# Cross-attention and feed-forward on one core: the order of the start of the attention phase is changed

## The reference

```python
x = x + xattn(layernorm(x), ctx_768, Wq, bq, Wk, bk, Wv, bv, Wo, bo)
x = x + ffn(layernorm(x), W1, b1, phases, w_real, w_imag, W2, b2)
# xattn: q = h@Wq+bq; k, v = ctx@Wk+bk, ctx@Wv+bv; 16 heads of 32
#   attn = softmax(clip(q k^T * 32**-0.5, -1e4, 1e4)); if any value is NaN: attn = 1/64 everywhere
#   (attn v) @ Wo + bo
# ffn: hidden = h@W1+b1; imag = w_imag*sin(phases + 0.1*hidden)
#   q = hidden + (cos(phases)*w_real + sin(phases)*w_imag)*imag*0.1;  relu(q)@W2 + b2
```

## Time and profile before

| | us |
|---|---|
| median of 3 runs (lowest, highest) | 2076.57 (2076.09, 2077.97) |
| profiled execution, its time | 2075.65 |
| profiled execution, span from first to last instruction | 2073.9 |
| mean granted clock of TensorE in it | 0.994 |
| busy in it: TensorE, VectorE | 2046.1, 1360.8 |
| busy in it: ScalarE, GpSimd | 1146.1, 1041.5 |

### The profile page before, as it was taken

The page is one execution under the profiler, slowest core; times in us unless marked ns, Lnnn a source line. Parts: engine busy times, 40 slices in busy tenths (PEclk is TensorE's granted clock), DMA queues, the critical chain, the costliest instruction groups (busy, mean ns, idle before and its releaser), DMA issues.

```text
span 2073.9 us, 27093 instructions
## 1 busy us (share of the span) xinstructions
PE 2046.1 (99%) x9738; PEld 1719.5 (83%) x9738; DVE 1360.8 (66%) x2037; ACT 1146.1 (55%) x2037; POOL 1041.5 (50%) x754
## 2 busy tenths in 40 slices
PE   6999999999999999999999999999999999999999
PEld 5888888888888888888888888888888888888887
DVE  6888888888876765555555555555656556565554
ACT  4666767767664655454554545545455444554543
POOL 3767777777776345344343433435434353343521
PEclk9899999999999999999999999999999999999999
DMA  5123223223213321211112111121111211112100
GB/s 183 57 77 104 90 82 113 82 87 97 72 62 111 114 76 37 72 41 41 44 49 71 41 41 41 51 72 41 41 41 52 71 41 41 41 48 75 37 26 21
DMA packets 133654, 133.93 MB, mean 65 GB/s; under 512 B 68872, under 2 KB 84744, under 8 KB 133520
## 3 DMA queue, kind: packets, MB, share of 16 engines
q1 hardware_dynamic: 132512, 132.16, 21.3%
q10 hardware_dynamic: 1008, 0.04, 0.0%
HBM read 81.83 MB, written 50.35 MB: 64 GB/s over the span
## 4 chain that ended last, share of the span: by engine, by line
PE 92%; DVE 3%; ACT 2%; issue 1%; DMA 1%; POOL 1%; SPq 0%; POOLq 0%; ACTq 0%; DVEq 0%
PE psum L1168 29%; PE psum L1170 29%; PE psum L1169 29%; PE psum L1251 3%; PE psum L1174 1%; DVE hid L1100 1%; DMA x_dram<-res 0%; ACT act_hi L836 0%; DVE act_lo L1103 0%; ACT hid L847 0%; POOL prob L606 0%; ACT frac L832 0%; DMA x_sb<-in_x 0%; ACT w_hi L684 0%; POOL q_lo L559 0%
## 5 line engine op out<-in xcount | busy, mean ns | idle before, releaser
L658 POOL TENSOR_TENSOR frac<-turns,frac 128x512 f32<-128x512 f32 x256 | 333.3, 1302 | 827.7 <-DVE frac L1128 827.7
L1100 DVE SCALAR_TENSOR_TENSOR hid<-frac,gain,hid 128x512 f32<-128x512 f32 x256 | 322.4, 1259 | 143.5 <-ACT frac L832 142.4
L1168 PE MATMUL psum<-w_hi,act_hi 128*128 128x512 f32 x1024 | 398.4, 389 | 0.9 <-DVE act_lo L1103 0.9
L1170 PE MATMUL psum<-w_hi,act_lo 128*128 128x512 f32 x1024 | 398.4, 389 | 0.0
L1169 PE MATMUL psum<-w_lo,act_hi 128*128 128x512 f32 x1024 | 398.3, 389 | 0.0
L836 ACT ACTIVATE act_hi<-hid 128x512 fp32r<-128x512 f32 x256 | 161.8, 632 | 356.3 <-DVE hid L1100 356.3
L845 ACT ACTIVATE turns<-psum,u_shift 128x512 f32<-128x512 f32 x256 | 176.5, 689 | 327.3 <-PE psum L1170 269.1
L1103 DVE SCALAR_TENSOR_TENSOR act_lo<-hid,act_hi 128x512 fp32r<-128x512 f32 x256 | 197.6, 772 | 178.8 <-ACT act_hi L836 178.8
L1128 DVE TENSOR_SCALAR frac<-turns 128x512 f32<-128x512 f32 x256 | 111.4, 435 | 248.5 <-ACT turns L845 248.5
L1168 PEld LDWEIGHTS psum<-w_hi,act_hi 128*128 128x128 f32 x1024 | 192.2, 188 | 41.0 <-issue 1.3
L1170 PEld LDWEIGHTS psum<-w_hi,act_lo 128*128 128x128 f32 x1024 | 192.3, 188 | 39.8
(11 more groups left out here) (158 smaller groups left out, 4199.8 us busy)
## 6 DMA issues: line engine op xcount, KB each, us to landing
res<-in_x SPq DMA_DIRECT2D x64, 256.0 KB, 2.9
x_dram<-res SPq DMA_DIRECT2D x64, 256.0 KB, 2.0
x_sb<-in_x SPq DMA_DIRECT2D x15, 1024.0 KB, 5.8
x_sb<-x_dram SPq DMA_DIRECT2D x15, 1024.0 KB, 5.6
xn<-turn_dram SPq DMA_DIRECT2D x30, 512.0 KB, 5.9
out<-x_sb SPq DMA_DIRECT2D x15, 1024.0 KB, 5.8
turn_dram<-stage SPq DMA_DIRECT2D x112, 128.0 KB, 2.4
stage<-in_w SPq DMA_DIRECT2D x32, 256.0 KB, 2.9
```

The lines of the kernel that those rows point to most:

```text
L658: pool.tensor_tensor(frac[:, j % 2, :], turns[:, j % 2, :], frac[:, j % 2, :], ALU.subtract)\
L1100: dve.scalar_tensor_tensor(out=hid[:, j % 2, :], in0=frac[:, j % 2, :], scalar=gain[:, f:f + 1], in1=hid[:, j % 2, :], op0=ALU.mult, op1=A ...
L1168: pe.matmul(o, a_hi, b_hi, start=first, stop=False)
L1170: return pe.matmul(o, a_lo, b_hi, start=False, stop=last)
```

## The change

- The sums of the context (for the mean value) are no longer taken from PSUM ahead of wk's low parts. They are taken in step 1 (`SUM_STEP`), one sum over the high parts and one over the low parts in SBUF, and added; a new tile `ctx_rest` holds the second. The small products of step 5 wait for them.
- wq's high parts are made by ScalarE, one behind each high part of tile 0, and no more by VectorE.
- keys(1) comes ahead of queries(0), values(0) behind it, both ahead of step 0; the other values move up a step. values(2) and values(3) use other banks, and waits on banks are renamed to fit.
- ScalarE takes keys_rows(1) and wv's high parts ahead of q_to_hi(0).
- VectorE reduces the phases and writes the rows of values(0) ahead of step 0, the phases in the same operations as before.
- The norm of tile 1 on ScalarE stands behind q_to_hi(2) and the exponential of step 1.
- wo's first block is split in step 3.

```diff
--- before.py
+++ after.py
@@ -99,8 +99,9 @@
 
 
 K_BANKS, K_STEPS = (2, 3, 7, 5), (None, None, 0, 1)
-V_BANKS, V_STEPS = (2, 6, 7, 6), (0, 1, 2, 3)
-WO_STEPS = (4, 4, 5, 5)
+V_BANKS, V_STEPS = (2, 6, 2, 7), (None, 0, 1, 2)
+SUM_STEP = 1
+WO_STEPS = (3, 4, 5, 5)
 M_BANK = U_BANK = 4
 
 Y2_BANK = NB
@@ -213,6 +214,7 @@
         total = sbuf(pa, "total", [P, 2, NB * HG])
         inv = sbuf(pa, "inv", [P, 2, NB * HG])
         ctx_sum = sbuf(pa, "ctx_sum", [P, KK, B])
+        ctx_rest = sbuf(pa, "ctx_rest", [P, KK, B])
         bv_sb = sbuf(pa, "bv_sb", [P, KC])
         vm_hi, vm_lo = (o[:, O_BUFS - 1, :].rearrange("p (k r b) -> p k r b", k=KC, b=B) for o in (o_hi, o_lo))
         wq_raw = prob[:].rearrange("p s h k -> p (s h k)")
@@ -754,11 +756,14 @@
             weights_to_hi(wk_hi, wk_sb, kw_in)
             for k in range(KC):
                 xt_to_hi(0, k, xt_bank(0, k))
+                act.wait_ge(wq_in[k], 16)
+                act.activation(wq_hi[:, k, :], wq_raw[:, k * C:(k + 1) * C], ACT.Copy, scale=SCALE)\
+                    .then_inc(w_hi_done, 1)
             keys_rows(0)
+            keys_rows(1)
             keys_to_hi(0, 0)
+            weights_to_hi(wv_hi, wv_sb, vw_in)
             q_to_hi(0)
-            keys_rows(1)
-            weights_to_hi(wv_hi, wv_sb, vw_in)
 
             for i in range(GROUPS + LAG_A):
                 t, g = divmod(i, KC)
@@ -779,8 +784,6 @@
                         if late and j == 0:
                             act.wait_ge(o_psum, late)
                         act.activation(pt_hi[:, j, :], psum[:, pt_bank(i, j), :], ACT.Copy).then_inc(pt_hi_done, 1)
-                if i == 1:
-                    layer_rows(1, range(NB))
                 if next_keys(i):
                     keys_to_hi(*next_keys(i))
                 if next_values(i):
@@ -791,6 +794,8 @@
                     act.wait_ge(shift_done, i + 1)
                     rows = prob[:, i % SCORE_BUFS]
                     act.activation(rows, rows, ACT.Exp).then_inc(exp_done, 1)
+                if i == 1:
+                    layer_rows(1, range(NB))
                 if i in K_STEPS:
                     keys_rows(K_STEPS.index(i))
                 if has_burst(i):
@@ -937,10 +942,6 @@
                 dve.tensor_tensor(ctxt_lo[:, k, :], psum[:, k, :], ctxt_hi[:, k, :].bitcast(F32), ALU.subtract)\
                     .then_inc(ctxt_lo_done, 1)
 
-            for k in reversed(range(KK)):
-                dve.reduce_sum(ctx_sum[:, k, :], psum[:, k, :].rearrange("p (b k) -> p b k", b=B), AX_X)\
-                    .then_inc(ctx_sum_done, 1)
-
             def keys_to_lo(b, g):
                 dve.wait_ge(kbd_hi_done, b * KC + g + 1)
                 dve.tensor_tensor(kbd_lo[:, g, :], k_masked[:].rearrange("p h k -> p (h k)"),
@@ -965,15 +966,30 @@
 
             weights_to_lo(wk_lo, wk_sb, wk_hi, 0)
             for k in range(KC):
-                dve.wait_ge(wq_in[k], 16)
-                raw = wq_raw[:, k * C:(k + 1) * C]
-                dve.tensor_scalar(wq_hi[:, k, :], raw, SCALE, None, ALU.mult).then_inc(w_hi_done, 1)
+                xt_to_lo(0, k, xt_bank(0, k))
                 dve.wait_ge(w_hi_done, k + 1)
-                dve.scalar_tensor_tensor(out=wq_lo[:, k, :], in0=raw, scalar=SCALE, in1=wq_hi[:, k, :].bitcast(F32),
-                                         op0=ALU.mult, op1=ALU.subtract).then_inc(w_lo_done, 1)
-                xt_to_lo(0, k, xt_bank(0, k))
+                dve.scalar_tensor_tensor(out=wq_lo[:, k, :], in0=wq_raw[:, k * C:(k + 1) * C], scalar=SCALE,
+                                         in1=wq_hi[:, k, :].bitcast(F32), op0=ALU.mult, op1=ALU.subtract)\
+                    .then_inc(w_lo_done, 1)
             keys_to_lo(0, 0)
             weights_to_lo(wv_lo, wv_sb, wv_hi, KK)
+
+
+            dve.wait_ge(par_in, 64)
+            reduce_phase(red[:, 1, :], theta, red[:, 0, :], 0)
+            dve.tensor_scalar(red[:, 2, :], red[:, 1, :], math.pi / 2, None, ALU.add).then_inc(par_step, 1)
+            dve.wait_ge(par_step, 6)
+            reduce_phase(red[:, 7, :], red[:, 2, :], red[:, 0, :], 6)
+            dve.tensor_scalar(red[:, 3, :], red[:, 1, :], PI_DOWN, -PI_DOWN, ALU.min, ALU.max)\
+                .then_inc(par_step, 1)
+            dve.tensor_scalar(red[:, 4, :], red[:, 7, :], PI_DOWN, -PI_DOWN, ALU.min, ALU.max)\
+                .then_inc(par_step, 1)
+            dve.wait_ge(par_step, PAR_REDUCED)
+            dve.scalar_tensor_tensor(out=red[:, 2, :], in0=bias1, scalar=0.1, in1=red[:, 1, :], op0=ALU.mult,
+                                     op1=ALU.add).then_inc(par_step, 1)
+            dve.wait_ge(par_step, PAR_REDUCED + 1)
+            dve.tensor_scalar(u_shift[:], red[:, 2, :], 1.0 / TWO_PI, None, ALU.mult).then_inc(par_step, 1)
+            values_rows(0)
 
             for i in range(STEPS_A):
                 t, g = divmod(i, KC)
@@ -1028,22 +1044,13 @@
                         xt_to_lo(t + 1, k, xt_bank(t + 1, k))
                 if i in V_STEPS:
                     values_rows(V_STEPS.index(i))
-                if i == 0:
-
-                    dve.wait_ge(par_in, 64)
-                    reduce_phase(red[:, 1, :], theta, red[:, 0, :], 0)
-                    dve.tensor_scalar(red[:, 2, :], red[:, 1, :], math.pi / 2, None, ALU.add).then_inc(par_step, 1)
-                    dve.wait_ge(par_step, 6)
-                    reduce_phase(red[:, 7, :], red[:, 2, :], red[:, 0, :], 6)
-                    dve.tensor_scalar(red[:, 3, :], red[:, 1, :], PI_DOWN, -PI_DOWN, ALU.min, ALU.max)\
-                        .then_inc(par_step, 1)
-                    dve.tensor_scalar(red[:, 4, :], red[:, 7, :], PI_DOWN, -PI_DOWN, ALU.min, ALU.max)\
-                        .then_inc(par_step, 1)
-                    dve.wait_ge(par_step, PAR_REDUCED)
-                    dve.scalar_tensor_tensor(out=red[:, 2, :], in0=bias1, scalar=0.1, in1=red[:, 1, :], op0=ALU.mult,
-                                             op1=ALU.add).then_inc(par_step, 1)
-                    dve.wait_ge(par_step, PAR_REDUCED + 1)
-                    dve.tensor_scalar(u_shift[:], red[:, 2, :], 1.0 / TWO_PI, None, ALU.mult).then_inc(par_step, 1)
+                if i == SUM_STEP:
+
+                    for context, sums in ((ctxt_hi, ctx_sum), (ctxt_lo, ctx_rest)):
+                        dve.reduce_sum(sums[:], context[:].bitcast(F32).rearrange("p k (b n) -> p k b n", b=B), AX_X)\
+                            .then_inc(ctx_sum_done, 1)
+                    dve.wait_ge(ctx_sum_done, 2)
+                    dve.tensor_tensor(ctx_sum[:], ctx_sum[:], ctx_rest[:], ALU.add).then_inc(ctx_sum_done, 1)
                 for k in range(KC):
                     if WO_STEPS[k] == i:
                         dve.wait_ge(w_hi_done, KC + k + 1)
@@ -1210,12 +1217,16 @@
             pe.wait_ge(xn0_done, 1)
             for k in range(KC):
                 transposes(0, k, xt_bank(0, k))
+            pe.wait_ge(ctxt_lo_done, KK)
             pe.wait_ge(kv_lo_done, KK)
-            pe.wait_ge(ctx_sum_done, KK)
             keys(0)
+            pe.wait_ge(xt_lo_done, 1)
+            keys(1)
             pe.wait_ge(w_lo_done, KC)
             queries(0)
-            keys(1)
+            pe.wait_ge(kv_lo_done, 2 * KK)
+            pe.wait_ge(kt_done, 1)
+            values(0)
 
             for i in range(STEPS_A):
                 t, g = divmod(i, KC)
@@ -1256,7 +1267,7 @@
                     if i == 1:
                         pe.wait_ge(kt_done, 2)
                     elif late == 0:
-                        pe.wait_ge(vn_done, 1)
+                        pe.wait_ge(vn_done, 3)
                     elif i == U_STEP + 1:
                         pe.wait_ge(u_done, 1)
                     elif has_burst(i - 1):
@@ -1286,15 +1297,15 @@
                         pe.wait_ge(q_full_done, 1)
                     keys(K_STEPS.index(i))
                 if i in V_STEPS:
-                    if i == 0:
-                        pe.wait_ge(kv_lo_done, 2 * KK)
-                        pe.wait_ge(kt_done, 1)
+                    if i == 1:
+                        pe.wait_ge(vn_done, 1)
                     elif i == 2:
                         pe.wait_ge(pt_lo_done, PAIRS)
                     values(V_STEPS.index(i))
                 if i == M_STEP:
 
                     pe.wait_ge(q_full_done, i + 1)
+                    pe.wait_ge(ctx_sum_done, 3)
                     for k in range(KC):
                         for kk in range(KK):
                             m = pe.matmul(psum[:, M_BANK, k * B:(k + 1) * B], wv_sb[:, kk, k * P:(k + 1) * P],
@@ -1331,8 +1342,6 @@
                         pe.wait_ge(vbd_lo_done, (lt // TPB) * KC + lg + 1)
                     if g == KC - 2 and i < GROUPS:
                         pe.wait_ge(q_full_done, i + 2)
-                    elif i == V_STEPS[3]:
-                        pe.wait_ge(vn_done, 3)
                     elif i == V_STEPS[3] + 1:
```

## The result

| | before | after |
|---|---|---|
| median, us (6 runs each, in turns) | 2076.33 | 2068.18 |
| ratio, 95% interval | | 0.9964 (0.9951 to 0.9977) |
| profiled execution, its time | 2075.65 | 2067.22 |
| its span | 2073.9 | 2065.4 |
| scores(0), scores(7) in it | 31.48, 107.03 | 25.70, 97.79 |

The change makes the kernel faster by 0.36%, some 7.5 us by the ratio (the two medians are 8.15 us apart). 2067.4 was forecast, with 2062.5 to 2072.3.

The account below looks back on a forecast made before the run. TensorE was taken as the bound, with 22.2 us of waits and half clock before scores(7), and VectorE tighter later. 22.2 - (10.65 + 2.3) = 9.2 us less gave 2066.4 profiled, 2067.4 as median, range 2062.5 to 2072.3.

Parts of the forecast that it names:

- parts 1 to 3: Start: sums off the path, wq's high parts on ScalarE, new order before step 0; scores(0) at 25.95 against 31.48.
- the 9.2 us: Total gain forecast from fewer waits and less half clock, almost all from the clock and step 2.
- Rival 1: Start: half clock till the end of queries(0), all behind later by 2.6 us, 2070.0; chance 0.14.
- part 4: Steps 0 to 2: scores(2) at 42.5 against 53.61, then a 2.2 us wait before tile 1's fourth transpose.
- the 5.20 us: TensorE's wait before the scores of step 2 in the kernel before, forecast to be gone.
- covered: Ahead of step 1: phase block in VectorE's idle time, covered up to 0.2 us; tile 2's load at 38.8, just covered.
- Steps 3 to 6: TensorE waits of 3.5 us in step 3, 2.6 in step 4, 0.4 each in steps 5 and 6.
- Rival 4: Waits follow each other, clock at 0.50 from 52 us to the end of step 5: slower, 2083; chance 0.05.
- Rival 2: Steps 2 to 5: VectorE isn't the bound, waits shrink by 2 to 5 us, 2063.5; chance 0.09.
- Rival 3: A new wait, tile 2 landing late or kt(3) holding POOL, costs 3 to 6 us, 2072; chance 0.10.

Follow-up runs that it names:

- experiment 8: Changed kernel with the context's sums taken from PSUM again ahead of wk's low parts, none in step 1: 2068.26 us, ratio to before 0.9968.
- experiment 12: Changed kernel with wq's high parts on VectorE again: 2068.70 us, ratio to before 0.9961.
- experiment 7: Changed kernel with the two sums of step 1 ahead of tile 2's statistics, in VectorE's wait for tile 2: 2065.64 us, ratio to before 0.9953.
- experiment 1: Changed kernel with the norm of tile 1 again ahead of q_to_hi(2) on ScalarE: 2066.63 us, ratio to before 0.9958.
- 2: Kernel before with the move of tile 1's norm alone: 2076.77 us, ratio to before 1.0001.
- Experiment 4: Kernel before with the phase block moved ahead of wv's low parts and tile 2's load ahead of the store of values(0): 2072.03 us, ratio 0.9984.
- experiment 9: Changed kernel with tile 2's load issued ahead of the store of values(0) on SP: 2066.31 us, ratio to before 0.9948.
- 3: Kernel before with only VectorE's phase block moved out of step 0, ahead of wv's low parts: 2076.10 us, ratio to before 0.9999.
- experiment 11: Changed kernel with wo's first block split in step 4 again: 2068.33 us, ratio to before 0.9960.
- 6: Changed kernel with the phase block back in step 0: 2068.31 us, ratio to before 0.9965.
- 5: Kernel before with the phase block early, tile 2's load first and the norm's move: 2070.12 us, ratio to before 0.9973.
- 10: Changed kernel with tile 2's load first and the sums ahead of its statistics: 2066.57 us, ratio to before 0.9949.

## Why the prediction was right, and where its steps were not

- **The start (parts 1 to 3) came as worked out.** Forecast and measured: keys 15.4, 15.13; queries(0) 20.2, 19.86; scores(0) 25.95, 25.70; the clock 1.00 throughout. 5.8 of the 9.2 us are there, and about 2.5 of them are the queries at full clock. Undone one at a time, the sums' move gives back 3.1 us of it (experiment 8) and wq's high parts 1.6 (12). The one miss is that a wait before the keys remains, 0.81 us, since the transposes ended at 14.3 rather than 15.3. Rival 1 didn't happen: the first product behind 28 transposes and a wait of 0.81 us ran with 0.30 and then 0.23 us to the next. The Trainium skill's rule on transposes ("TensorE: Matmul & The Clock Gate", Part 4: PE-mode transpose) would have given rival 1; the trace disagrees here too.
- **The sums** were taken at 1.8 each and cost 1.74; that they stand on VectorE's path in step 1 is shown by experiment 7. So what the sums' move wins at the start it pays again in step 1 (experiment 8).
- **The step that failed is in part 4**: "the norm of tile 1 ... now stands behind exp(1) ... and the 5.20 us are gone". The wait did go, but the norm's move is not what the gain comes from: undone, it costs nothing (experiment 1), and alone it brings nothing (2). A wait of TensorE in step 2 had behind it a chain with three members in one place: the phase block on VectorE, ScalarE's order, and tile 2's load, which SP issues only behind the store of values(0). Taking one away uncovers the next. What the runs point to is the early values(0), which lets SP go on to tile 2 at 34.4 instead of 46.5, beside either of the others. That is argued, not shown: no run undoes the early values(0), and none moves tile 2's load alone in the kernel before. Experiment 4, which gets tile 2 early in another way and moves the phase block, takes 5.8 us from steps 0 to 6 of the kernel before in its profile (some 2.6 of them by a clock that did not fall) and 3.3 us by the times. My sum had both in it as things "covered", and gave their gain to the norm.
- **Tile 2's load was mis-sized.** I had it end at 38.8, as 11.7 us behind the rows of values(0); it ended at 42.6, because the store took 3.0 us rather than 2.2 to land, the load 8.2 rather than 5.9, and the rows of values(0) were done 0.7 us later, behind a phase block of 4.2 us for 3.5. It cost 1.3 us, by experiment 9, and not more, since VectorE had to wait for values(2) in any case; total came at 47.97 for 47.1, and the wait before the fourth transpose was 3.15 for 2.2.
- **Steps 3 to 6** came as worked out in kind: 2.94 and 1.58 us for 3.5 and 2.6, half clock from 64.4 behind the first of them, then behind the small products. Behind the 3.15 us wait of step 2, where I expected 0.50 too, the clock stayed at 1.00. Waits 9.5 for 10.65 and clock 3.4 for 2.3 are two errors of 1.1 that cancel, so that 9.24 us at scores(7) meets the 9.2 of the sum is in part luck; scores(7) at 97.8 for 98.
- **Behind scores(7)** I let everything move by as much. 0.7 us of it was lost there, at the start of the feed-forward, and up to 4.4 us in other executions (1971.3 against 1966.9 us).
- **Rival 4** (half clock from 52 us on) was far off: the slow stretch in steps 3 and 4 lasted 3.4 us. **Rival 2** (VectorE not the bound) fell: TensorE still waits 7.9 us for VectorE in steps 2 to 5. **Rival 3** had the right place, tile 2, but not the price: 1 us, not 3 to 6.

## What to carry to other kernels

A wait in a trace names what came last, not what the time is worth: before giving a gain to a move, ask what the next member of the chain (another engine's block, a transfer queued behind a store) would end at, and try the move alone. Small work of no urgency belongs where an engine waits for a transfer, not behind it: the same two sums cost 3.3 us behind the wait and nothing in it (steps 0 to 6 took 68.75 us with them there, 68.83 without them in experiment 8). And an early loss can be paid twice where the clock falls behind it: 1.8 us of sums ahead of the first keys cost 3.1 us at scores(0) (experiment 8), while wq's high parts on VectorE, 1.7 us with the clock at 1.00 behind them, cost 1.6 (experiment 12).

## What I had not expected of the hardware

The phase block took 4.2 us in the changed kernel, 3.5 before. Here is one of its operations on 16 numbers a lane (L923), first in 0.18 us and on its second pass in 1.14, and the one behind it, which took 0.17 on its first pass, in 0.54:

```profile
23.28 0.18 DVE L923 SCALAR_TENSOR_TENSOR red<-red,par 128x16 f32<-128x16 f32 x1
...
24.54 1.14 DVE L923 SCALAR_TENSOR_TENSOR red<-red 128x16 f32<-128x16 f32 x1
25.71 0.54 DVE L926 SCALAR_TENSOR_TENSOR red<-red 128x16 f32<-128x16 f32 x1
```

GpSimd's at the same time:

```profile
24.34 1.30 POOL L561 TENSOR_TENSOR q_lo<-q_full,q_hi 128x512 fp32r<-128x512 f32 x1 [5.09 <-ACT q_hi L721]
25.61 0.61 POOL L546 TENSOR_TENSOR k_masked<-kt,mask_k 128x256 f32<-128x256 f32 x1
```

The two slow ones ended when GpSimd's operations did, at 25.6 and 26.2. The Trainium skill, "SBUF — State Buffer", section "SBUF: two separate sides", says that an operation of VectorE with two SBUF inputs and one of GpSimd that reads SBUF exclude each other for their whole length; this trace agrees. The small addition of the sums did the same in experiment 7 (0.96 us beside GpSimd, 0.18 in the changed kernel). It was hidden there.

The load of tile 2 (1024 KB each time) took 5.9 us before and 8.2 after, behind the same reloads and chunks in SP's order, and between 5.8 (experiments 3 and 11) and 8.3 (6) in kernels whose order of DMAs was the same. What makes it slow in one execution I have not found; against scores(0), VectorE's total of step 1 lay 1.3 us earlier in experiment 11 than in the changed kernel, and that is as much as some of the edits are worth.

The clock fell at different times behind nearly the same start. Experiments 2 to 5 waited 3.13, 2.78, 3.04 and 2.25 us before the first keys. In 3 and 5 the clock was 0.50 from 17 to 19 us; in 2 and 4, with the longer waits, it was 1.00 there and fell at about 23.2 and 22.6. From queries(0) to scores(0) it then took 7.3 and 7.4 us in 3 and 5, where the clock was back at 1.00 sooner, and 8.3 in 2, 4 and the kernel before. Where the wait before the first keys was 0.6 to 1.6 us, in the changed kernel and in experiments 1, 6, 7 and 9 to 12, the clock stayed at 1.00 to scores(0), in 12 even behind 2.21 us before queries(0); behind 1.89 us (experiment 8) it fell at 18.3.
